# Spreading B's rows over the partitions in a Mamba scan: DMA and ScalarE in place of TensorE

## The reference, cut to what matters

```python
def _mamba(x, in_w, conv_w, conv_b, xproj_w, dt_w, dt_b, A_log, D, out_w):
    ...                                   # u, z: projections; u: 4-tap convolution and silu
    dbc = u @ xproj_w.T                   # 64 columns for dt, 16 for B, 16 for C
    dt = softplus(dbc[..., :dt_rank] @ dt_w.T + dt_b)
    Bm = dbc[..., dt_rank:dt_rank + d_state]
    Cm = dbc[..., dt_rank + d_state:]
    A = -jnp.exp(A_log)
    dA = jnp.exp(dt[..., None] * A)
    dBu = (dt * u)[..., None] * Bm[:, :, None, :]
    def step(h, inp):
        dA_t, dBu_t, C_t = inp
        h = dA_t * h + dBu_t
        return (h, jnp.einsum('bdn,bn->bd', h, C_t))
    ...                                   # scan over the 2048 tokens
    return y * silu(z) @ out_w.T          # y = scanned + u * D
```

## Time and profile before

| | us |
|---|---|
| median of 3 runs | 1368.16 |
| lowest and highest | 1364.99 and 1369.56 |
| span of the profiled execution | 1397.4 |
| scan stage in it, from the first scan to the end of the last | 42.0 to 804.4 |

### The profile page before, as it was taken

One profiled execution on the slowest core, in us unless ns is written; L12 is line 12 of the kernel. 1 busy time (PEld: TensorE's weight loads), 2 busy tenths in 40 slices (PEclk: granted clock), 3 DMA queues, 4 the chain that ended last, 5 costly groups with the idle time before them and its releaser, 6 DMA issues.

```text
span 1397.4 us, 27753 instructions
## 1 busy us (share of the span) xinstructions
PE 1272.1 (91%) x9894; PEld 962.1 (69%) x9894; DVE 1097.7 (79%) x1829; ACT 947.2 (68%) x1630; POOL 1013.4 (73%) x620
## 2 busy tenths in 40 slices
PE   6799999999999999999998779999989999986695
PEld 2567767676777676766766646689966666656693
DVE  5799999999999999999999953333357888874475
ACT  5888988898889888988988842245545555532243
POOL 2789999999999999999999916223334665664442
PEclk9999999999999999999999999999999999998798
DMA  5545434543444454444444351312152000021223
GB/s 187 145 131 161 138 139 118 161 149 129 139 139 165 133 150 139 164 132 152 139 146 111 114 216 47 90 44 86 56 157 86 2 1 1 13 64 34 79 72 100
DMA packets 153014, 154.73 MB, mean 111 GB/s; under 512 B 96624, under 2 KB 121712, under 8 KB 143168
## 3 DMA queue, kind: packets, MB, share of 16 engines
q1 hardware_dynamic: 148112, 143.16, 32.8%
q0 software_dynamic: 4768, 9.81, 2.2%
HBM read 138.66 MB, written 20.20 MB: 114 GB/s over the span
## 4 chain that ended last, share of the span: by engine, by line
PE 49%; ACT 21%; DVE 16%; issue 8%; another core or an unknown queue 2%; DMA 2%; POOL 1%; SPq 1%; DVEq 1%; POOLq 0%; ACTq 0%
DVE hh L887 7%; PE pq L410 6%; ACT da L720 6%; PE pa L506 4%; PE py L525 3%; ACT pa L725 3%; PE bank L1562 3%; PE bank L1558 2%; PE pr L2016 2%; PE bank L1572 2%; PE pr L2219 2%; PE pr L2030 2%; PE bank L1478 2%; DVE hh L897 2%
## 5 line engine op out<-in xcount | busy, mean ns | idle before, releaser
L1042 POOL TENSOR_TENSOR hc<-hh,cs 128x1024 f32<-128x1024 f32 x256 | 596.9, 2369 | 24.6 <-DVE hh L887 21.7
L887 DVE TENSOR_TENSOR_SCAN hh<-da,st,pa 128x512 f32<-128x512 f32 x240 | 292.7, 1261 | 14.1 <-PE pa L506 12.6
L525 PE MATMUL py<-ident,hc 128*128 128x128 f32 x2048 | 268.4, 277 | 7.4 <-ACT yt L738 5.8
L525 PEld LDWEIGHTS py<-ident,hc 128*128 128x128 f32 x2048 | 229.1, 141 | 54.4 <-issue 29.1
L506 PEld LDWEIGHTS pa<-dg,dtut 64*128 64x128 f32 x2560 | 160.9, 189 | 107.0 <-issue 103.2
L506 PE MATMUL pa<-dg,dtut 64*128 64x128 f32 x2560 | 189.8, 285 | 29.6 <-DVE hh L887 20.6
L720 ACT ACTIVATE da<-dt,w 128x512 f32<-128x512 f32 x320 | 209.7, 711 | 0.2
L897 DVE TENSOR_TENSOR_SCAN hh<-pa,st,hh 128x512 f32<-128x512 f32 x144 | 175.2, 1265 | 6.1 <-POOL hh L1032 3.7
L725 ACT ACTIVATE pa<-dt,w 128x512 f32<-128x512 f32 x192 | 124.5, 680 | 35.2 <-DVE hh L887 20.8
L410 PE MATMUL pq<-xn,w 128*128 128x512 f32 x248 | 124.6, 627 | 3.6 <-ACT xn L755 3.6
L1032 POOL TENSOR_TENSOR hh<-dtu,bs 128x1024 f32<-128x1024 f32 x48 | 112.8, 2365 | 3.1 <-issue 1.9
(11 more groups left out here) (341 smaller groups left out, 2643.8 us busy)
## 6 DMA issues: line engine op xcount, KB each, us to landing
cs<-bcrows SPq DMA_DIRECT2D x64, 1024.0 KB, 4.9
dg<-blocks SPq DMA_DIRECT2D x80, 256.0 KB, 5.0
bs<-bcrows SPq DMA_DIRECT2D x48, 256.0 KB, 3.7
blocks<-bcrows SPq DMA_DIRECT2D x320, 1.0 KB, 3.2
xsorted<-in_pads SPq DMA_DIRECT2D x13, 387.0 KB, 5.7
rot<-in_rot SPq DMA_DIRECT2D x4, 1024.0 KB, 4.9
wx<-in_l_w SPq DMA_DIRECT2D x4, 1024.0 KB, 10.0
ysort<-ytoken SPq DMA_DIRECT2D x14, 256.0 KB
```

Of the source, the lines that this page charges most:

```text
L525: i = pe.matmul(py[:, h * CH + kt * P:h * CH + (kt + 1) * P], hc[s % HCS][:, h, t], ident[:, :], is_transpose=True, start=n == 0 and kt == ...
L887: v.tensor_tensor_scan(hh[(NS * m + nj) % HHS][:, h, :], da[q % DAS][:, :], inflows, 0.0 if first else st[:, m % 2, nj, h:h + 1], ALU.mult ...
L1042: g.tensor_tensor(hc[s % HCS][:, :, :], hh[s % HHS][:, :, :], cs[j % 2][:, s % CG, :].unsqueeze(1).broadcast_to([P, HF, CH]), ALU.mult).th ...
```

## The change

B's rows for VectorE's three inflows no longer come from TensorE. `b_row_in` loads each from DRAM, spread over the partitions, into one of four buffers `brow` (128 x 512 each); `spread_b` is now ScalarE's and copies the buffer into `pb`. Per unit three matrix products go, and three DMAs of 256 KB and three copies of 128 x 512 come. ScalarE's copy waits for its row, for VectorE's inflow before (which has read `pb`) and for its own `keep_dtu`. The constant `sel` and its load go, and with them one count of 16 on a semaphore of small loads. `keep_rows` no longer waits for the products. The four semaphores of the row loads are used again by a later stage, whose counts therefore start at `back0`.

```diff
-SLOTS, DAS, BG = 4, 4, 2
+SLOTS, DAS, BG, BVS = 4, 4, 2, 4
...
+        s_back = [sem(f"b_row_in_then_back_in{i}") for i in range(4)]
+        back0 = 16 * (UNITS * len(BY_V) // BVS)
...
+            s_brow = s_back
...
-                sel = sb(k, "sel", [P, NS])
+                brow = [sb(k, f"brow{i}", [P, CH]) for i in range(BVS)]
...
-                    def spread_b(s):
-                        m, n = s // NS, s % NS
-                        if made(BY_V, s) >= 2:
-                            pe.wait_ge(s_db, made(BY_V, s) - 1)
-                        pe.wait_ge(s_turnk, turned_count(m, HF - 1))
-                        pe.matmul(pb[:, :], sel[:, n:n + 1].broadcast_to([P, P]), crow[m % 2][:, :], start=True, stop=True).then_inc(s_b, 1)
-
...
-                        if s + 2 < STEPS and by_vector(s + 2):
-                            spread_b(s + 2)
                         if s + 1 < STEPS and by_pe(s + 1) and n not in (LAG + 1, 10, 11):
                             inflow(s + 1)
...
-                            act.wait_ge(s_b, len(BY_V) * (m - 1))
...
+                    def spread_b(s):
+                        m = s // NS
+                        k = made(BY_V, s) - 1
+                        act.wait_ge(s_brow[k % BVS], 16 * (k // BVS + 1))
+                        if k >= 1:
+                            act.wait_ge(s_db, k)
+                        act.wait_ge(s_turnk, turned_count(m, HF - 1))
+                        act.activation(pb[:, :], brow[k % BVS][:, :], ACT.Identity).then_inc(s_b, 1)
+
...
                         if s % NS == LAG and s >= NS:
                             keep_sum(s // NS - 1)
+                        if s + 2 < STEPS and by_vector(s + 2):
+                            spread_b(s + 2)
                         ahead = s + 1 < STEPS and by_pe(s + 1) and BY_P.index((s + 1) % NS) % 2 and (s + 1) % NS < 10
...
+                    def b_row_in(k):
+
+                        m = k // len(BY_V)
+                        sy.wait_ge(s_cout, 16 * (m + 1))
+                        if k >= BVS:
+                            sy.wait_ge(s_b, k - BVS + 1)
+                        sy.dma_start(brow[k % BVS][:, :], bcrows[m][BY_V[k % len(BY_V)], :].partition_broadcast(P)).then_inc(s_brow[k % BVS], 16)
+
...
                     load_block(0)
+                    for i in range(len(BY_V)):
+                        b_row_in(i)
...
                             b_in(m + 1, 0)
                             for i in range(2):
+                                b_row_in((m + 1) * len(BY_V) + i)
+                            for i in range(2):
                                 diagonals_out((m + 1) * len(PAIRS) + i)
                         c_in(4 * m + 3)
                         if m + 1 < UNITS:
+                            b_row_in((m + 1) * len(BY_V) + 2)
                             for i in range(2, len(PAIRS)):
                                 diagonals_out((m + 1) * len(PAIRS) + i)
```

More of the change, by code:

```diff
@@ L214, in layer0_mamba @@
             s_dtu = sem("dtu_made")
-            s_b, s_db, s_gdb = sem("b_spread"), sem("inflow_by_vector"), sem("inflow_by_gpsimd")
+            s_b, s_db, s_gdb = sem("b_rows_in_psum"), sem("inflow_by_vector"), sem("inflow_by_gpsimd")
+            s_brow = s_back
             s_pin = sem("inflow_by_tensor")
@@ L558, in mamba_tensor @@
                     pe.wait_ge(s_xv, 2)
-                    pe.wait_ge(s_small, 80)
+                    pe.wait_ge(s_small, 64)
                     pe.wait_ge(s_slot, slot_count(turn["relu", 0, HF - 1]))
@@ L769, in mamba_scalar @@
                     roots(range(0, 4), 1)
-                    act.wait_ge(s_small, 80)
+                    act.wait_ge(s_small, 64)
                     keep_turned(0)
@@ L976, in mamba_vector @@
                     rows(2)
-                    v.wait_ge(s_small, 80)
+                    v.wait_ge(s_small, 64)
                     keep_turned(1)
@@ L1050, in mamba_gpsimd @@
                         count["ng"] += 4
-                    g.wait_ge(s_small, 80)
+                    g.wait_ge(s_small, 64)
                     inflow(0)
@@ L1075, in mamba_sync @@
                             sy.dma_start(keep[:, :], a["keep"]).then_inc(s_small, 16)
-                            sy.dma_start(sel[:, :], a["sel"]).then_inc(s_small, 16)
                             sy.dma_start(number[:, :], a["number"]).then_inc(s_small, 16)
@@ L1190, in build @@
         s_xsort, s_scat, s_ret = sem("sorted_in"), sem("scattered"), sem("returned")
-        s_back = [sem(f"back_in{i}") for i in range(4)]
         s_back0 = sem("first_back_in")
@@ L2109, in final_tensor @@
                     for q in (6, 7):
-                        pe.wait_ge(s_back[q % 4], 16 * B + 16 * (q // 4) + 16)
+                        pe.wait_ge(s_back[q % 4], back0 + 16 * B + 16 * (q // 4) + 16)
                         pe.matmul(summed(q), ident[:, :], back1[:, piece(q), :], start=False, stop=True).then_inc(s_yo, 1)
@@ L2116, in final_added @@
                     else:
-                        v.wait_ge(s_back[q % 4], 16 * B + 16 * (q // 4) + 16)
+                        v.wait_ge(s_back[q % 4], back0 + 16 * B + 16 * (q // 4) + 16)
                         v.tensor_tensor(bx[:, piece(q), :], x1[:, piece(q), :], back1[:, piece(q), :], ALU.add).then_inc(s_iadd, 1)
@@ L2538, in experts_in @@
                         else:
-                            v.wait_ge(s_back[chunks[0] // 4], 16 * B)
+                            v.wait_ge(s_back[chunks[0] // 4], back0 + 16 * B)
                         for t in tiles:
@@ L2821, in constants @@
     k["centre"] = np.eye(D, dtype=np.float32) - np.float32(1.0 / D)
-    k["sel"] = (np.arange(P)[:, None] == np.arange(NS)).astype(np.float32)
     k["before"] = np.triu(np.ones((P, P), np.float32), 1).astype(mybir.dt.np(BF16))
```

## The result

The changed kernel takes **1444.88 us** (1436.96 to 1447.45) beside 1368.86 us for the kernel before in the same runs: ratio **1.0546, interval [1.0508, 1.0584]**, slower. The forecast was 1431 us, in a range of 1402 to 1452.

A forecast was written before the change was run, and what follows sets the result against it. Bound: a chain of waits, mid-unit ScalarE's program order twice, with VectorE waiting. Fourteen units at 4.30 (60.2), first unit 2.5 and last 0.5 sum to 63.2 us on the median 1368.2: 1431 us, range 1402 to 1452.

The forecast's parts named there:

- The stalls: VectorE waits for ScalarE's late copies before the inflows of steps 4 and 10: 2.27 and 2.4 us per unit.
- step 13 without a stall: Copy for step 13, behind ScalarE's last square: VectorE asks only after its first softplus step, so no wait.
- Removing TensorE's products at nothing: Three one-hot products per unit, at most 3.1 us, gain nothing because TensorE then waits for VectorE's scans.
- hiding the loads: The 48 row loads of 256 KB are issued 20 us or more before the unit needing them, so cost nothing.
- The term for the unit: Each of fourteen units takes 51.99 us in place of 47.69, 4.30 more, 60.2 us in all.
- a case of its own: Rival: TensorE's clock falls in each unit around its longer idle, adding 1.7 us per unit, 1456 us; chance 0.10.
- First unit: Most of the step 4 delay already there, the step 10 delay applies, later dg loads about 1: 2.5 us.
- Last unit: No next unit prepared, SiLU half as long, step 4's exponentials one copy later: 0.5 us.
- Adding the difference to the median unscaled: Whole kernel: 63.2 us added to the median 1368.2, though the profiled span is 29 us longer; scaled, 62.
- GpSimd as the bound: Rival: both copies in time, TensorE's relief closes GpSimd's idle, 16 units by 1.1 us faster, 1350 us; chance 0.04.
- TensorE as the bound: Rival: the whole removal of TensorE's products is gained, 49 us faster, 1319 us; chance 0.02.
- One stall only: Rival: VectorE's second delay is absorbed, leaving 2.07 us by 15, 31 us, 1399 us; chance 0.06.

The follow-up runs named there:

- the filler: Changed kernel plus 16 TensorE products of a tile of noughts per unit, right behind the sums of step 6: 1439.89 us, ratio 1.0486.
- the single moves: Changed kernel with one copy issued earlier: step 4's ahead of the SiLU, 1425.83 us; or step 10's in step 6, 1409.64 us.

## Why the prediction was right, and where it was off

**The mechanism and the unit.** Right to 0.2 us at each point of the unit shown. With t = 0 at the inflow of step 12 (555.90 in that unit; 607.83 is the next):

| Point of the chain | Forecast t | Measured t |
|---|---|---|
| VectorE's inflow of step 4 | 23.42 | 23.29 |
| exponentials of step 7 | 32.31 | 32.18 |
| copy for step 10 | 42.29 | 42.17 |
| inflow of step 10 | 42.98 | 42.78 |
| scan of step 9 | 44.10 | 43.92 |
| next inflow of step 12 | 51.99 | 51.93 |

The stalls were forecast at 2.27 and 2.4 and measured at 2.2 and 2.7, the copy at 0.59 and measured at 0.58, step 13 without a stall. Removing TensorE's products at nothing was right (the kernel without copies), and so was hiding the loads in every unit but the first.

**The term for the unit: 4.30 forecast, 5.04 measured**, 14 x 0.74 = 10.4 us. The step that failed is that the forecast put TensorE's clock at nothing, as a case of its own with a chance of 0.10. By the filler's units the two waits were worth 4.1, so their term was 0.2 too large, and the clock added some 0.9 to it: it came true beside the forecast and not in its place. The prediction had one idle place and its length right (3 us ahead of the inflow of step 11) and saw that the rows lie on both sides of a fall; it had only two outcomes, 0.2 and 1.7 us in all units. What came is a fall in every unit, in some of them at the inflow of step 5, an idle place that it had not looked at. It is not the same in all units: the seven with a mean clock of 0.97 take 51.99 us and the other seven 1.2 us more (53.16).

The prediction also misread its row for 3.10 us of idle. It saw the next inflow take 1.16 us and went no further. This is TensorE's next row in the kernel before:
```profile
797.24 1.52 PE L521 MATMUL py<-ident,pre 128*128 128x128 f32 x8
```
The same eight products took 1.03 us at 87.18, and from 798 to 801 the granted clock is 0.50. So the clock had fallen behind 3.10 us of idle as well, only one inflow later, and the chance of 0.10 was too small by the prediction's own trace.

**First unit: 2.5 forecast (1 to 4.5), 6.5 measured** (57.10 to 50.62 us). The mis-sized term is "three issues before the first dg loads may cost about 1": the 16 small writes behind them take longer too, and the load comes 4.0 us later on the queue. That these 4.0 us are the whole miss is argued and not shown. In all eight kernels here that load the rows early, the load comes 17.4 to 18.9 us behind the first, but their first units take from 52.1 to 57.1 us, and TensorE's clock in them differs too (0.93 to 0.88).

**Last unit: 0.5 forecast, 2.0 measured** (from the last SiLU to the end of the last scan 39.61 before, 41.62 after). ScalarE's and VectorE's timelines show a copy that stands behind two more things in the last unit, a table load and square roots:
```profile
841.93 1.28 ACT L175 ACT_TABLE_LOAD   x1
843.22 0.47 ACT L175 ACTIVATE pq<-moments,eps 128x16 f32<-128x16 f32 x2
843.63 0.58 ACT L728 ACTIVATE pb<-brow 128x512 f32<-128x512 f32 x1
```
```profile
844.29 1.22 DVE L872 TENSOR_TENSOR hh<-dtu,pb 128x1024 f32<-128x1024 f32 x1 [2.92 <-issue]
```
I had read that VectorE waits there anyway; the inflow ahead of that wait now waits itself.

**The sum.** 10.4 + 4.0 + 1.5 = 15.9 us too little in the scan stage (78.1 measured, with the first SiLU 1.0 us earlier, for 63.2 forecast): the whole missed 1444.88 by 14 us. Adding the difference to the median unscaled was right, since the 29 us by which the profiled execution was longer lay behind the scan stage. The measured time is 2 us above the 1420 to 1443 that the prediction's own bounds gave. It lies in the range because that went on to 1452, with no term worked out for the upper part: that much was luck.

**The rivals.** GpSimd as the bound, faster if both copies came in time: refuted, since even without any copies the unit is 47.55 us. TensorE as the bound: refuted by the same run. One stall only: refuted by the sums of the single moves.

## What to carry to other kernels

Where engines run fixed programs in order, price an operation by what stands ahead of it on its new engine and by when its reader asks, not by its own time: three copies of 0.58 us cost 5 us per unit in one order (some 4 of it the waits, the rest TensorE's clock behind them), and two of them nothing in another. Write both times down before the move; their difference was the stall to 0.3 us here. And ask why the reader asks so early: its inflow stood ahead of the scan to fill a wait of its own, so moving it behind gave back only half.

## What the runs showed of the hardware

- VectorE's product of two SBUF operands took between 1.2 and 5.6 us (3.29 in the case shown, beside GpSimd's products), and GpSimd's next product grew from 2.40 to 3.36 us; with one operand in PSUM VectorE's took 1.20 to 1.22 us each time shown.
- Sixteen small writes behind three loads of 256 KB on the same queue took 13.7 us to issue, and 11.3 or 10.9 without them.
- Idle times of TensorE of the same length (2.92 and 2.93 us) left it with 2.08 or 1.81 us for the next inflow and 3.78 or 2.96 us for the products behind it; idle of 2.12 and 2.09 us was followed by an inflow of 2.04 us in one unit and of 1.16 us in another, and idle of 3.10 us by an inflow of 1.16 us with the granted clock at 0.50 from 0.7 us behind its end.
